# State-space stages of a decoder: softplus chain and row norms on ScalarE and GpSimd, C product one state later, four buffers

## Chip, cores and metric

One core of a Trainium2 chip runs the whole program. The metric is the time of one execution in device microseconds; the engines are TensorE (PE in the profile, PEld its weight loads), VectorE (DVE), ScalarE (ACT), GpSimd (POOL) and SyncE (SP, which issues the DMAs).

## What is computed

The program is a decoder of four layers (twelve blocks) over x of 128 sequences x 64 positions x 128 channels. The change touches one block, the attention of layer 2, which is a selective state-space layer run forwards (m1) and backwards (m2). For each direction, on h = layernorm(layernorm(x)):

```python
xs, z = jnp.split(jnp.einsum('bld,ed->ble', x, in_w), 2, axis=-1)      # 256 channels each
xs = silu(causal_conv_4_taps(xs) + conv_b)
dt, Bc, Cc = jnp.split(jnp.einsum('bld,ed->ble', xs, xproj_w), [8, 24], axis=-1)   # 16 states
dt = jax.nn.softplus(jnp.einsum('blr,dr->bld', dt, dt_w) + dt_b)
dA = jnp.exp(dt[..., None] * A)
dBx = dt[..., None] * Bc[:, :, None, :] * xs[..., None]
# scan over the positions: h = dA_t * h + dBx_t;  y = sum over states of h * C_t
y = (y + Dp * xs) * silu(z)
return jnp.einsum('bld,od->blo', y, out_w)
```

## The kernel before

`mamba` (L1689) is called twice, with `first` true for m1. It works on 16 groups (`C.NG`) of 512 rows (8 sequences of 64 positions). The 256 channels are two halves of 128 partitions (`NHF` 2), the 512 rows lie along the free axis. A group has 16 states (`NS`). All engines run their own hand-written instruction streams, ordered by semaphores; each has a loop of 8 turns with two groups in a turn.

The work of state s of a group:

- GpSimd `state` multiplies `dtx` (dt times xs) by the row of B into `dBx[s % 2]` (L1793), 128x1024. B's rows are spread over the partitions by SyncE's DMAs (`spread_B`, L1757), two states to a transfer, four slots.
- ScalarE `state` makes the decays exp(A dt) into PSUM (`ps_dA`, L1960), one 128x504 activation for each half. There are three such banks, so it can be three halves ahead of the scan and no more.
- VectorE `state` (L2072) runs a scan for each half (L2077), drains, waits for C and multiplies the state by C's row in `ps_C` into `yc[s % 2]` (L2083).
- TensorE waits for `yc`, then spreads C of the next state (`spread_C`, L1872, one bank) and adds `yc` to `ps_y` with four matmul instructions by the identity (`add_state`, L1887).

Beside state s of group i each engine has `front(i + 1, s, ...)`, the preparation of the next group, spread over the states by number. TensorE: gate products at s 2, low-rank products at 3, step sizes (`dt_done`) at 6, transposes at 8, convolution at 10 to 13. ScalarE: silu(z) at 4, copies of `low` and `parts` at 6, exp at 9, copy of rows at 10, ln and exp at 12; silu of xs between states 0 and 1 (`activate`). VectorE: the three-part split of C at 5 (L2044 to L2050), bias, x and -|x| at 7 (L2054, L2057), max(x, 0) and (e+1)-1 at 10 (L2060, L2061), x + ln at 12 (L2065), the last subtraction at 13 (L2069); row normalisation (`normalise`, L2033) at 4 and, in m1, the first normalisation into Y at 14 (L2105). GpSimd: two products of the softplus correction at 11 and 12 and `dtx` at 15. `AHEAD = 2` states of the next group are done at the end of a group. Between them VectorE multiplies `ps_y` by silu(z) (L2109) and adds the projected rows to Y (L2112).

On every engine the order within a state is first `state(i, s)`, then `front(i + 1, s)`, except on TensorE, where `front(i + 1, s)` comes first and then the wait for `yc` of state s:

```python
                        front(i + 1, s, 1 - par, True)
                        if s == 9:
                            skip(par)
                        pe.wait_ge(yc_ready, i * NS + s + 1)
                        spread_C(to, its)
                        add_state(s)
```

## Time and profile before

| | us |
|---|---|
| median of 3 runs | 11680.44 (11670.45 to 11685.3) |
| the profiled execution | 11666.28 |
| its span, first to last instruction | 11664.5 |
| m1, from its first load to that of m2 | 4701.85 to 6062.85 |
| m2, to the start of the joining stage | 6062.85 to 7383.65 |

Busy over the whole span are TensorE 74%, VectorE 67%, ScalarE 34% and GpSimd 21%, but twelve blocks with different limits are mixed in this. The change is confined to 4701.85 to 7383.65 us, so only that stretch is to be read. There a timeline of each engine and the table of waits are the useful views: a row of the timeline gives start, duration, engine, line, operation, names and count, and in brackets the idle time before it and what ended it.

### The profile page before, as it was taken

To read this page: it belongs to the slowest core of one execution; us is meant where nothing else is said; L and a number is where in the kernel's file an instruction comes from. 1 tells how busy PE (TensorE), PEld (TensorE's weight loads), DVE (VectorE), ACT (ScalarE), POOL (GpSimd) and SP (SyncE) were. 2 spreads that over 40 slices of the span, in tenths; PEclk is the share of its full clock that TensorE was granted. 3 is DMA by queue.
4 is the path that set the end of the run, shared out by engine and by line. 5 is a ranking of instruction groups with operands and counts; after the bars stand their busy time and mean duration, and the time that the engine had idled before them with its cause. 6 is when DMAs were issued, how large, how long until landed. Compare 5 with 4: busy or idle time off the path is not lost. (4 is left out here: it accounts for less than half of the span.)

```text
span 11664.5 us, 161252 instructions
## 1 busy us (share of the span) xinstructions
PE 8604.9 (74%) x60164; PEld 5385.6 (46%) x60164; DVE 7794.8 (67%) x11203; ACT 3961.3 (34%) x5327; POOL 2427.5 (21%) x805
## 2 busy tenths in 40 slices
PE   5666888756766747677767777788668888876789
PEld 4444555433445432232223333455445666664566
DVE  6655324567777864788878888555775666666644
ACT  3333213311111025444444444533333333333333
POOL 0000000025445620455545555100000000000000
PEclk7777666667767767888888888899669999997589
DMA  0000000000000000111111111000000000000000
GB/s 18 0 9 7 4 1 0 1 14 0 0 0 0 0 8 0 50 51 52 53 46 53 56 53 55 11 11 8 0 0 17 2 2 2 2 6 6 6 8 14
DMA packets 83306, 183.24 MB, mean 16 GB/s; under 512 B 16107, under 2 KB 38231, under 8 KB 82199
## 3 DMA queue, kind: packets, MB, share of 16 engines
q1 hardware_dynamic: 82966, 178.64, 4.7%
q8 instruction: 223, 3.65, 0.1%
q14 instruction: 117, 0.95, 0.0%
HBM read 171.20 MB, written 7.41 MB: 15 GB/s over the span
## 5 line engine op out<-in xcount | busy, mean ns | idle before, releaser
L1784 POOL TENSOR_TENSOR m_dBx<-m_dtx,m_Bs 128x1024 f32<-128x1024 f32 x516 | 1246.9, 2419 | 863.0 <-DVE m_hs L2077 840.0
L2077 DVE TENSOR_TENSOR_SCAN m_hs<-m_ps_dA,m_dBx 128x512 f32<-128x512 f32 x1032 | 1203.0, 1207 | 189.9 <-POOL m_dBx L1784 139.2
L1889 PE MATMUL m_ps_y<-m_yc,ident 128*128 128x512 f32 x2064 | 1197.1, 711 | 0.0
L1960 ACT ACTIVATE m_ps_dA<-m_dt,m_A 128x504 f32<-128x504 f32 x1032 | 689.1, 679 | 1387.6 <-DVE m_hs L2077 1377.0
L2418 PE MATMUL x_ps_p<-Y,ident 128*128 128x256 f32 (+1 forms) x1920 | 713.5, 547 | 384.4 <-DVE Y L2335 214.8
L2418 PEld LDWEIGHTS x_ps_p<-Y,ident 128*128 128x128 f32 x1920 | 425.7, 242 | 664.7 <-issue 241.5
L2083 DVE TENSOR_TENSOR m_yc<-m_hs,m_ps_C 128x1024 f32<-128x1024 f32 x516 | 630.2, 1221 | 96.4 <-issue 88.0
L1872 PE MATMUL m_ps_C<-m_parts,m_sel 128*128 128x512 bf16 x518 | 229.1, 442 | 616.5 <-DVE m_yc L2083 615.9
L1889 PEld LDWEIGHTS m_ps_y<-m_yc,ident 128*128 128x128 f32 x2064 | 465.5, 227 | 379.3 <-issue 355.4
L547 POOL MEMSET c_vbd<- 128x1152 f32 x2 | 2.1, 1062 | 2939.5 <-POOLq L56 2939.5
L2341 POOL TENSOR_TENSOR Y<-x_score,x_v 128x1024 f32<-128x1024 f32 (+1 forms) x72 | 471.8, 6585 | 243.1 <-DVE x_most L2721 159.6
L1872 PEld LDWEIGHTS m_ps_C<-m_parts,m_sel 128*128 128x128 bf16 x518 | 51.2, 99 | 1007.0 <-DVE m_yc L2083 971.6
L352 PE MATMUL c_ps_t<-ident,c_s 128*128 128x128 f32 x1024 | 238.6, 394 | 233.5 <-ACT c_s L526 233.5
L2341 DVE TENSOR_TENSOR Y<-x_score,x_v 128x1024 f32<-128x1024 f32 (+1 forms) x72 | 375.7, 5254 | 4.3 <-PE x_ps_p L2418 4.3
L2335 POOL TENSOR_TENSOR Y<-x_qk 128x2048 f32<-128x2048 f32 x48 | 305.4, 6392 | 102.8 <-DVE x_most L2711 89.2
L352 PEld LDWEIGHTS c_ps_t<-ident,c_s 128*128 128x128 f32 x1024 | 173.1, 201 | 266.7 <-issue 224.7
L352 PE MATMUL a_ps_t<-ident,a_s 128*128 128x128 f32 x1024 | 218.1, 367 | 87.6 <-ACT a_s L526 87.6
L1127 PEld LDWEIGHTS f_ps_o<-f_w,f_hid 128*128 128x128 f32 x2048 | 246.4, 192 | 65.9 <-issue 46.0
L1339 PE MATMUL a_ps_o<-a_pT,a_val 64*64 64x128 f32 x4096 | 257.9, 277 | 19.3 <-ACT a_pT L1436 19.3
L1324 PE MATMUL a_ps_t<-ident,a_s 128*128 128x128 f32 x1024 | 141.7, 283 | 165.6 <-DVE a_s L1481 152.0
L526 ACT ACTIVATE c_s<-c_s 128x2048 f32<-128x2048 f32 x64 | 122.1, 1908 | 412.3 <-DVE c_s L631 412.3
L1352 PE MATMUL a_ps_out<-a_wo,a_oT 128*128 128x128 f32 x2048 | 256.5, 280 | 0.0
(690 smaller groups left out, 19445.1 us busy)
## 6 DMA issues: line engine op xcount, KB each, us to landing
m_Bs<-m_B_rows SPq DMA_DIRECT2D x258, 512.0 KB, 3.6
c_kvb<-in_ctxT SPq DMA_DIRECT2D x50, 256.0 KB, 2.5
out_dram<-X SPq DMA_DIRECT2D x1, 4096.0 KB
m_B_rows<-m_low SPq DMA_DIRECT2D x34, 32.0 KB, 3.2
c_table<-in_table SPq DMA_DIRECT2D x2, 512.0 KB
focus_rows<-X SPq DMA_DIRECT2D x2, 512.0 KB, 9.5
x_xb<-in_ctx SPq DMA_DIRECT2D x1, 1024.0 KB, 14.8
x_xa<-focus_rows SPq DMA_DIRECT2D x1, 1024.0 KB, 7.1
```

The source lines that it names most:

```text
L352: last = nc.tensor.transpose(ps_t[:, m % 2, t * P:(t + 1) * P], s1[:, u, m // 2, h:h + 2, :].rearrange("p h k -> p (h k)"), C.ident[:])
L1339: last = nc.tensor.matmul(ps_o[r, t, :].rearrange("p (j q) -> p j q", q=P)[:, js, S * b:S * b + S], val[r, q, hg * NK + k, :], pT[r, t, js ...
L1352: last = nc.tensor.matmul(ps_out[:, t, :], oT[:, t, j, :], wo[:, hg * NJ + j, :], start=hg == 0 and t == 0 and j == 0, stop=end and not cr ...
L1784: return nc.gpsimd.tensor_tensor(to, one, other, ALU.mult)
L1872: nc.tensor.matmul(ps_C[:], sel[:, s, :], parts[:, par, :], start=True, stop=True).then_inc(C_done, 1)
L1889: last = nc.tensor.matmul(ps_y[:, m, :], C.ident[:], yc[:, s % 2, m, :], start=s == 0, stop=s == NS - 1)
L1960: nc.scalar.activation(seqs(ps_dA[:, h % 3, :]), seqs(dt[:, par, m, :]), ACT.Exp, scale=A[:, m, s:s + 1]).then_inc(decay, 1)
L2077: nc.vector.tensor_tensor_scan(h[:, m, :], ps_dA[:, (2 * s + m) % 3, :], dBx[:, s % 2, m, :], 0.0, ALU.mult, ALU.add).then_inc(scanned, 1)
L2083: nc.vector.tensor_tensor(yc[:, s % 2, :, :], h, bc(ps_C[:].unsqueeze(1), both), ALU.mult).then_inc(yc_ready, 1)
L2335: return eng.tensor_tensor(to.rearrange("p (q k d) -> p q k d", q=queries, k=ck), bc(qk[:, 0, q:q + queries, :].unsqueeze(2), [P, queries, ...
L2341: last = eng.tensor_tensor(to[:, r * ck * D:(r + 1) * ck * D].rearrange("p (h e k) -> p h e k", h=NH, e=HD), bc(s[:, q + r, :, :].unsqueez ...
L2418: last = nc.tensor.matmul(sum_bank(c)[:, 0:width], C.ident[:], parts[:, :, e], start=e == 0, stop=e == n - 1)
```

## The change

Ring sizes: `AHEAD` goes from 2 to 3, `dBx` and `hs` get four buffers each in place of two, `ps_dA` keeps three banks and `yc` two. VectorE's `state` is split in `scan(j, s)` and `weigh(j, s)`; `weigh` of state s - 1 stands behind `scan` of state s, without a drain. Softplus: TensorE's sums are read by ScalarE (Abs and Relu with the bias, at s 7), exp(-|x|) and 1 + e at 8, ln, 1 - v and exp(-ln) at 9; GpSimd does the four sums and products that follow at s 10 to 13 and `dtx` at 14. `normalise` and the first normalisation become ScalarE activations (s 6 and 13). TensorE's gate products move from s 2 to 3 and the low-rank products from 3 to 4; ScalarE's copies move from 6 to 5. Initial marks are written to a small tile, and ScalarE waits for `scaled` at the start.

```diff
@@ sizes
-    AHEAD = 2
-    SLOTS, CHUNK = 4, 2
-    FREE_HALVES, FREE_STATES = 3, SLOTS * CHUNK
+    AHEAD = 3
+    SLOTS, CHUNK, BX, HS = 4, 2, 4, 4
+    FREE_HALVES, FREE_STATES, FREE_ROWS = 3, SLOTS * CHUNK, 1
...
-        dBx, hs, yc = (sb(n, [P, 2, NHF, GT]) for n in ("dBx", "hs", "yc"))
+        dBx = sb("dBx", [P, BX, NHF, GT])
+        hs, yc = sb("hs", [P, HS, NHF, GT]), sb("yc", [P, 2, NHF, GT])
@@ gpsimd
-                pool.wait_ge(scanned, j * (2 * NS) + (2 * s - 2 + FREE_HALVES))
+                if s >= BX or not in_prologue:
+                    pool.wait_ge(scanned, j * (2 * NS) + (2 * s - 2 * BX + 2 + FREE_HALVES))
...
-                if s == 11:
-                    pool.wait_ge(v_ready, j + 1)
+                if s == 10:
+                    pool.wait_ge(excess, j + 1)
                     hold()
-                    nc.gpsimd.tensor_tensor(v[:], v[:], e[:], ALU.subtract)
+                    nc.gpsimd.tensor_tensor(v[:], v[:], e[:], ALU.add)
                     pool.drain()
+                elif s == 11:
+                    multiply(v[:], v[:], r[:])
                 elif s == 12:
-                    pool.wait_ge(r_ready, j + 1)
-                    hold()
-                    multiply(v[:], v[:], r[:]).then_inc(excess, 1)
-                elif s == 15:
-                    pool.wait_ge(dt_ready, j + 1)
-                    hold()
+                    nc.gpsimd.tensor_tensor(dt[:, par, :, :], x[:], ln[:], ALU.add)
+                    pool.drain()
+                elif s == 13:
+                    nc.gpsimd.tensor_tensor(dt[:, par, :, :], dt[:, par, :, :], v[:], ALU.add).then_inc(dt_ready, 1)
+                    pool.drain()
+                elif s == 14:
                     multiply(dtx[:, par, :, :], dt[:, par, :, :], xs[:, par, :, :])
@@ tensor
-                if s == 2:
+                if s == 3:
                     gate(j, 0)
...
-                elif s == 3:
+                elif s == 4:
                     low_products(j, par)
...
-                        pe.wait_ge(yc_ready, i * NS + s + 1)
+                        pe.wait_ge(yc_ready, i * NS + (s + 1 + FREE_ROWS))
@@ scalar
+            def normalise(j):
+                for p in range(TPG):
+                    n = j * TPG + p
+                    last = nc.scalar.activation(xn[:, p, :], C.X[:, n, :], ACT.Identity, scale=C.RS2[:, bass.ds(n, 1)],
+                                                bias=C.NM2[:, bass.ds(n, 1)])
+                last.then_inc(xn_ready, 1)
...
-                elif s == 6:
+                elif s == 5:
                     act.wait_ge(dbl_done, j + 1)
...
+                elif s == 7:
+                    act.wait_ge(dt_done, j + 1)
+                    for m in range(NHF):
+                        nc.scalar.activation(e[:, m, :], bank[m][:], ACT.Abs, bias=dt_b[:, m:m + 1])
+                    for m in range(NHF):
+                        last = nc.scalar.activation(x[:, m, :], bank[m][:], ACT.Relu, bias=dt_b[:, m:m + 1])
+                    last.then_inc(x_ready, 1)
+                elif s == 8:
+                    act.drain()
+                    nc.scalar.activation(e[:], e[:], ACT.Exp, scale=-1.0)
+                    act.drain()
+                    nc.scalar.activation(v[:], e[:], ACT.Identity, bias=1.0)
                 elif s == 9:
-                    act.wait_ge(neg_ready, j + 1)
-                    nc.scalar.activation(e[:], e[:], ACT.Exp).then_inc(e_ready, 1)
+                    act.drain()
+                    nc.scalar.activation(ln[:], v[:], ACT.Ln)
+                    act.drain()
+                    nc.scalar.activation(v[:], v[:], ACT.Identity, scale=-1.0, bias=1.0)
+                    nc.scalar.activation(r[:], ln[:], ACT.Exp, scale=-1.0).then_inc(excess, 1)
                 elif s == 10:
                     copy_rows(j + 1)
-                elif s == 12:
-                    act.drain()
-                    nc.scalar.activation(ln[:], e[:], ACT.Ln, bias=1.0)
-                    act.drain()
-                    nc.scalar.activation(r[:], ln[:], ACT.Exp, scale=-1.0).then_inc(r_ready, 1)
-
+                elif s == 6 and in_loop:
+                    act.wait_ge(xT_done, j + 1)
+                    normalise(j + 1)
+                elif s == 13 and first and in_loop:
+                    first_norm(j - 1)
@@ vector
+            def scan(j, s, in_prologue=False):
+                if s >= HS or not in_prologue:
+                    dve.wait_ge(yc_ready, j * NS + (s - HS + 1 + FREE_ROWS))
                 dve.wait_ge(dBx_ready, j * NS + (s + 1 + FREE_STATES))
...
+            def weigh(j, s, wait_free=True):
+                dve.wait_ge(scanned, j * (2 * NS) + (2 * s + NHF + FREE_HALVES))
                 if wait_free:
                     dve.wait_ge(y_added, j * NS + (s - 1))
                 dve.wait_ge(C_done, j * NS + (s + 1))
...
                     for s in range(AHEAD, NS):
-                        state(i, s)
+                        scan(i, s)
+                        weigh(i, s - 1)
                         front(i + 1, s, 1 - par)
...
-                    state(i + 1, 0)
+                    scan(i + 1, 0)
+                    weigh(i, NS - 1)
+                    scan(i + 1, 1)
                     dve.wait_ge(y_added, i * NS + NS)
                     nc.vector.tensor_tensor(q[:], sz[:, par, :, :], ps_y[:], ALU.mult).then_inc(y_ready, 1)
-                    state(i + 1, 1)
+                    weigh(i + 1, 0)
+                    scan(i + 1, 2)
+                    weigh(i + 1, 1)
                     dve.wait_ge(out_done, i + 1)
```

In VectorE's stream the blocks for s 7, 10, 12 and 13, both normalisations and the drain at the end of a turn are gone; only the split of C at s 5 is left in its `front`.

## Rows read from the trace of the kernel before

**Rows 1.** The page: its first line, then busy time of each engine.
```profile
span 11664.5 us, 161252 instructions
PE 8604.9 (74%) x60164; PEld 5385.6 (46%) x60164; DVE 7794.8 (67%) x11203; ACT 3961.3 (34%) x5327; POOL 2427.5 (21%) x805
```
**Rows 2.** Table of waits, 4757 to 6060 us: total us, times, longest.
```profile
ACT m_ps_dA L1960 <- DVE m_hs L2077: 709.1, 312, 6.2
POOL m_dBx L1784 <- DVE m_hs L2077: 440.6, 192, 5.7
DVE m_hs L2077 <- POOL m_dBx L1784: 69.7, 34, 5.2
```
**Rows 3.** VectorE's timeline: L2109, first and last of 16, in m1, then m2.
```profile
4837.80 1.21 DVE L2109 TENSOR_TENSOR m_e<-m_sz,m_ps_y 128x1024 f32<-128x1024 f32 x1
...
6052.89 1.22 DVE L2109 TENSOR_TENSOR m_e<-m_sz,m_ps_y 128x1024 f32<-128x1024 f32 x1
6197.64 1.22 DVE L2109 TENSOR_TENSOR m_e<-m_sz,m_ps_y 128x1024 f32<-128x1024 f32 x1
...
7373.89 1.22 DVE L2109 TENSOR_TENSOR m_e<-m_sz,m_ps_y 128x1024 f32<-128x1024 f32 x1
```
**Rows 4.** VectorE's timeline in one group of m1.
```profile
5009.10 2.33 DVE L2077 TENSOR_TENSOR_SCAN m_hs<-m_ps_dA,m_dBx 128x512 f32<-128x512 f32 x2
5011.61 1.22 DVE L2083 TENSOR_TENSOR m_yc<-m_hs,m_ps_C 128x1024 f32<-128x1024 f32 x1 [0.18 <-issue]
5012.75 2.33 DVE L2077 TENSOR_TENSOR_SCAN m_hs<-m_ps_dA,m_dBx 128x512 f32<-128x512 f32 x2
...
5022.15 0.69 DVE L2044 TENSOR_TENSOR m_low<-m_ps_j,m_parts 64x512 f32<-64x512 f32 x1
...
5024.83 2.34 DVE L2077 TENSOR_TENSOR_SCAN m_hs<-m_ps_dA,m_dBx 128x512 f32<-128x512 f32 x2
...
5088.39 2.34 DVE L2077 TENSOR_TENSOR_SCAN m_hs<-m_ps_dA,m_dBx 128x512 f32<-128x512 f32 x2 [3.19 <-issue]
```
**Rows 5.** ScalarE's timeline in the same group, the front of state 12.
```profile
5048.86 1.28 ACT L1992 ACT_TABLE_LOAD   x1
5050.16 1.06 ACT L1992 ACTIVATE m_ln<-m_e 128x1024 f32<-128x1024 f32 x1
5051.27 1.28 ACT L1994 ACT_TABLE_LOAD   x1
5052.56 1.06 ACT L1994 ACTIVATE m_r<-m_ln 128x1024 f32<-128x1024 f32 x1
5053.52 1.87 ACT L1960 ACTIVATE m_ps_dA<-m_dt,m_A 128x504 f32<-128x504 f32 x3
```
**Rows 6.** Timeline of m1's start: a table load ahead of a wait, the first scan.
```profile
4732.49 1.28 ACT L1987 ACT_TABLE_LOAD   x1
...
4740.55 1.06 ACT L1987 ACTIVATE m_e<-m_e 128x1024 f32<-128x1024 f32 x1 [6.77 <-DVE m_e L2057]
...
4756.99 2.34 DVE L2077 TENSOR_TENSOR_SCAN m_hs<-m_ps_dA,m_dBx 128x512 f32<-128x512 f32 x2 [5.16 <-POOL m_dBx L1784]
```
**Rows 7.** Groups by line: Silu, m1 (busy, mean ns); then one line's instructions, Relu elsewhere.
```profile
L1978 ACT ACTIVATE m_sz<-m_ps_j 128x512 f32<-128x512 f32 x16 | 9.6, 597 | 0.2
L1047 ACT ACTIVATE f_hid<-f_ps_h,f_wib x64: 687/687/687, 1289.6 to 1650.1; 128x512 f32<-128x512 f32 x64
```
**Rows 8.** TensorE's timeline: the same four instructions at both clocks.
```profile
5044.11 1.88 PE L1889 MATMUL m_ps_y<-m_yc,ident 128*128 128x512 f32 x4
...
5075.77 3.62 PE L1889 MATMUL m_ps_y<-m_yc,ident 128*128 128x512 f32 x4
```
**Rows 9.** GpSimd's timeline: two products in a row; one behind a drain.
```profile
4754.62 4.64 POOL L1784 TENSOR_TENSOR m_dBx<-m_dtx,m_Bs 128x1024 f32<-128x1024 f32 x2 [0.26 <-issue]
...
5049.79 2.36 POOL L1784 TENSOR_TENSOR m_dBx<-m_dtx,m_Bs 128x1024 f32<-128x1024 f32 x1 [0.31 <-issue]
```
**Rows 10.** ScalarE's timeline in the joining stage: row normalisations, 128x128 with two pointer operands.
```profile
7385.26 3.18 ACT L2135 ACTIVATE mj_xn<-X,NM,RS 128x128 f32 x8
```

More of the change, by code:

```diff
@@ L1768, in _ @@
             store_B(C.NG, 0)
-            spread_B(C.NG, 0, 0)
+            for c in range((AHEAD + CHUNK - 1) // CHUNK):
+                spread_B(C.NG, 0, c)
         n_prepared = 2
@@ L1784, in multiply, with state @@
                 return nc.gpsimd.tensor_tensor(to, one, other, ALU.mult)
-            def state(j, s, par):
+            def state(j, s, par, in_prologue=False):
                 slot = s // CHUNK % SLOTS
@@ L1911, in _ @@
                 front(-1, s, 1, False)
-            for s in range(2, 14):
+            for s in range(3, 14):
                 front(0, s, 0, False)
@@ L1937, in _ @@
             for m in range(NHF):
-                nc.tensor.matmul(ps_y[:, m, :], C.ident[:], yc[:, 1, m, :], start=False, stop=True)
+                nc.tensor.matmul(ps_y[:, m, :], C.ident[:], yc[:, (AHEAD - 1) % 2, m, :], start=False, stop=True)
         @block.scalar
@@ L1947, in _, with first_norm @@
             seqs = lambda t: t.rearrange("p (s n) -> p s n", n=S)[:, :, 1:]
+            def normalise(j):
[4 more added lines that the diff above has]
+                last.then_inc(xn_ready, 1)
+            def first_norm(i):
+                for p in range(TPG):
+                    n = i * TPG + p
+                    last = nc.scalar.activation(C.Y[:, n, :], C.X[:, n, :], ACT.Identity, scale=C.RS[:, bass.ds(n, 1)],
+                                                bias=C.NM[:, bass.ds(n, 1)])
+                last.then_inc(Y_ready, 1)
             def copy_rows(j):
@@ L2012, in _ @@
                     activate(i + 2, par, True)
-                    state(i + 1, 1, 1 - par)
+                    for s in range(1, AHEAD):
+                        state(i + 1, s, 1 - par)
         @block.vector
@@ L2031, in _ @@
             dve.drain()
-            def normalise(j):
-                for p in range(TPG):
-                    n = j * TPG + p
-                    last = nc.vector.tensor_scalar(xn[:, p, :], C.X[:, n, :], C.RS2[:, bass.ds(n, 1)],
-                                                   C.NM2[:, bass.ds(n, 1)], ALU.mult, ALU.add)
-                last.then_inc(xn_ready, 1)
             def front(j, s, par):
@@ L2076, in state @@
                     dve.wait_ge(decay, j * (2 * NS) + (2 * s + m + 1))
-                    nc.vector.tensor_tensor_scan(h[:, m, :], ps_dA[:, (2 * s + m) % 3, :], dBx[:, s % 2, m, :], 0.0, ALU.mult,
-                                                 ALU.add).then_inc(scanned, 1)
-                dve.drain()
+                    nc.vector.tensor_tensor_scan(hs[:, s % HS, m, :], ps_dA[:, (2 * s + m) % 3, :], dBx[:, s % BX, m, :], 0.0,
+                                                 ALU.mult, ALU.add).then_inc(scanned, 1)
+            def weigh(j, s, wait_free=True):
+                dve.wait_ge(scanned, j * (2 * NS) + (2 * s + NHF + FREE_HALVES))
                 if wait_free:
@@ L2082, in state @@
                 dve.wait_ge(C_done, j * NS + (s + 1))
-                nc.vector.tensor_tensor(yc[:, s % 2, :, :], h, bc(ps_C[:].unsqueeze(1), both), ALU.mult).then_inc(yc_ready, 1)
-            normalise(0)
-            dve.drain()
-            dve.wait_ge(xT_done, 1)
-            normalise(1)
-            for s in range(5, 14):
-                front(0, s, 0)
+                nc.vector.tensor_tensor(yc[:, s % 2, :, :], hs[:, s % HS, :, :], bc(ps_C[:].unsqueeze(1), both),
+                                        ALU.mult).then_inc(yc_ready, 1)
+            front(0, 5, 0)
             for s in range(AHEAD):
-                state(0, s, False)
+                scan(0, s, True)
+                if s:
+                    weigh(0, s - 1, False)
             with dve.Fori(0, C.NG // 2) as pair:
@@ L2096, in _ @@
                     for s in range(AHEAD, NS):
[L2097 removed]
+                        scan(i, s)
+                        weigh(i, s - 1)
                         front(i + 1, s, 1 - par)
[L2099 to L2107 removed]
+                    scan(i + 1, 0)
+                    weigh(i, NS - 1)
+                    scan(i + 1, 1)
                     dve.wait_ge(y_added, i * NS + NS)
                     nc.vector.tensor_tensor(q[:], sz[:, par, :, :], ps_y[:], ALU.mult).then_inc(y_ready, 1)
[L2110 removed]
+                    weigh(i + 1, 0)
+                    scan(i + 1, 2)
+                    weigh(i + 1, 1)
                     dve.wait_ge(out_done, i + 1)
+                    if first:
+                        dve.wait_ge(Y_ready, i + 1)
                     nc.vector.tensor_tensor(rows(C.Y, i), ps_k[:].rearrange("p (t d) -> p t d", d=D), rows(C.Y, i),
                                             ALU.add).then_inc(out_read, 1)
[L2114 removed]
+            weigh(C.NG, AHEAD - 1)
 def mamba_join(C, name):
```

58 lines of the change are left out of this document (17 added, 41 removed).

## The prediction

> **What bounds the kernel now.** The page gives 67% for VectorE over the span [rows 1], a mean over twelve blocks; only the two state-space stages matter. I read the table of waits of m1 first. ScalarE and GpSimd wait for VectorE's scans for 709 and 441 us, VectorE for GpSimd for 70 us [rows 2]: VectorE is the engine that the others follow. Then VectorE's timeline. L2109 runs once a group, so its starts give the period: (6052.89 - 4837.80) / 15 = 81.0 us in m1 and (7373.89 - 6197.64) / 15 = 78.4 us in m2 [rows 3]. A state takes 12.75 - 9.10 = 3.65 us: two scans 2.33, a hole of 0.18 behind the drain, the product with C 1.14 from start to start [rows 4]. 16 x 3.65 = 58 us; the other 20 to 23 us of a group are VectorE's share of the front, GpSimd's late dBx (70 / 16 = 4.4) and, once in two groups, 3.19 us at the turn of the loop [rows 4].
>
> **What is taken from VectorE.** The drain goes: 2 x 1.13 + 1.14 = 3.40 a state, 54.4 a group. Left are the split of C (5024.83 - 5022.15 = 2.7 [rows 4]), the product L2109 (1.1 to the next start [rows 3]) and the row add L2112, half its elements (0.6, estimated from that row). VectorE's own work falls to 54.4 + 2.7 + 1.1 + 0.6 = 58.8 us a group. If it stayed the bound, that would be the period. The question is what waits end late instead, and I go by the order of each queue.
>
> **How far ScalarE may be away.** `ps_dA` still has three banks; only `dBx` and `hs` have become deeper. The second decay of state s can start when the first scan of state s - 1 ends (call it t). From t VectorE has the second scan, a product, two scans and a product of its own, 1.13 + 1.14 + 2.26 + 1.14 = 5.67, less 0.07 of overlap: it wants the first decay of state s + 1 at t + 5.60. ScalarE spends 0.05 + 0.62 on the second decay of s and 0.69 + 0.06 on that of s + 1 (duration and spacing from the three in a row [rows 5]; 0.05 to 0.07 is the hand-over between engines). So about 4.2 us of front per state are free. What exceeds it stops the scans. Four places exceed it:
>
> **(a) Silu of z, s 4.** The gate products now come at TensorE's s 3, after the matmuls of state 2, whose product on VectorE now stands behind the scans of state 3. It ends at t + 2.28. TensorE then spreads C (0.07 + 0.23), adds the state (1.72) and does two gate products (1.72, latency 0.16; four instructions start to start are 1.71 at the full clock [rows 8]): z is done at t + 6.18. Behind it on ScalarE come one silu (0.05 + 0.60 [rows 7]), a table load (0.02 + 1.28 [rows 5]) and the decay (0.75): t + 8.9 against 5.6, **3.3 us** of stall. The load of the silu table itself is hidden, since a load is executed ahead of the wait: 4732.49 against 4740.55 [rows 6]. Before, gate was at s 2 and its input one product earlier, so nothing waited.
>
> **(b) Step sizes, s 7.** VectorE read them before; now ScalarE does, and its decays of state 8 are queued behind. By the same steps (product of state 5, C, add, `dt_w` products) `dt_done` is at t + 6.18; then 0.05, two Abs and two Relu at 0.60 from start to start (0.687 each [rows 7]), the decay 0.75: t + 9.4 against 5.6, **3.8 us**.
>
> **(c) exp, ln, exp(-ln), s 8 and 9.** After (b) VectorE starts each scan as its decay comes, so all ScalarE's work counts: from scan 8's first start 0.5 to the end of the second decay, drain 0.1, exp 1.04, drain 0.1, 1 + e 0.95, two decays 1.3, load 1.28 + 0.1, ln 1.06, drain 0.1, 1 - v 1.06, load 1.28, exp 0.95, decay 0.75: 10.7 us until scan 10 can begin [rows 5]. VectorE needs 2 x 3.40 = 6.8: **3.9 us**.
>
> **(d) GpSimd, s 10 to 14.** Its queue stands at s 10 waiting for `excess`, which comes 0.6 us before scan 10; `dBx` 10 is the last it has made, so the four buffers are empty of anything ahead. From there each state needs a dBx and a front operation: 2.32 + 2.35 + 0.31 behind a drain [rows 9], 4.98 a state (4.64 for the one without a drain), against VectorE's 3.40. dBx 11 is 1.1 late, then 1.2 and 3 x 1.6: **7.1 us**. GpSimd's total, 21 operations or 50 us, fits in a group; its late start doesn't. Every moved sum counts here: before, three operations stood in this queue, now five.
>
> **(e) Silu of xs, states 0 and 1.** Two loads and two silus between two decays (3.9 us), with one scan less of allowance (`back` is 2 for the first two halves): **0.9 us**.
>
> The row norms are covered: 3.18 / 8 = 0.40 each [rows 10], 1.6 us at s 6 and at s 13, under the 4.2 us. Their cover gone, they would cost 1.6. Moving the copies to s 5 only follows the low products (0.5 wait, behind (a)). SyncE's stores and spreads have the first need of B's next rows 50 us after the copy; nothing is queued behind them. The bigger AHEAD lets three dBx be made at the group's end, which refills GpSimd's ring before scan 0.
>
> Sum: 3.3 + 3.8 + 3.9 + 7.1 + 0.9 = 19.0; 58.8 + 19.0 = 77.8. The turn of the loop stays, 3.19 less the drain's share of some 0.4, over two groups 1.4: 79.2. **The clock:** TensorE is now inside (a) and (b). [...] That costs between 0 and 3.65 us at each of (a) and (b), 7.3 in all; I take 3.0, nearer to nothing in (a), about 2 in (b). **Period 82.2 us, in both stages**, since Y's norm (m1 only) is no longer VectorE's.
>
> Against before: 15 x (82.2 - 81.0) + 15 x (82.2 - 78.4) = 18 + 57 = 75. The prologue is a bare chain: four norms ahead of the first copy (1.6), Abs and Relu against bias and negation, a table load that was hidden behind a wait [rows 6], two more ScalarE passes, four GpSimd operations of 2.35 to 2.66 in place of two and two on VectorE: I get the first scan 10.5 us later than now (4756.99 [rows 6]); the end has one more state to close, 3.5. 2 x 14 = 28. Total +103 on the profiled execution's 11666.28. The median of the runs is 14.2 above that: **11783 us**.
>
> [...] Rows first: each of ln and exp(-ln) has its own load of 1.28 us [rows 5]. [...]
>
> **Rivals.**
> - *The stalls at their least (same time).* TensorE stays at the full clock where it counts: period 79.2, 15 x (-1.8 + 0.8) + 28 = +13, 11693. [...]
> - *ScalarE's waits are covered (faster).* If the gate and step-size products are done before ScalarE asks, because VectorE's product of the state before is issued sooner than I place it, (a) and (b) vanish: it decides when they are done by t + 2.9 and t + 2.4 in place of t + 6.2. Period 79.2 - 7.1 = 72.1: 15 x (-8.9 - 6.3) + 28 = -200, 11480. With all stalls gone it would be 60.2 and 11120. For it: VectorE loses over 15 us of work a group. Against: three banks.
> - *TensorE slow in both chains (much slower).* All of 7.3: period 86.5, 15 x (5.5 + 8.1) + 28 = +232, 11912.
> - *The change does not do what it says*: the wait merely moves from VectorE's front to its decays; at equal periods only the 28 us of both ends are left, 11708. This lies between the first two cases of the sum and takes no chance of its own.
>
> **How the numbers follow.** My forecast (periods 80.5 to 84.5, that is 11732 to 11852) 0.60; least stalls 0.16; covered waits 0.16; slow chains 0.08. A measurement of this kernel can tell 0.2%, 23 us, from no change: 11657 to 11704 counts as the same. Slower is 0.60 + 0.08 = 0.68, the same 0.16, faster 0.16. The range of 8 in 10 leaves out the covered waits and half of the slow chains: 11650 to 11880.
>
> **What would show it.** In the table of waits of m1 VectorE's scans should wait for the decays (L1960's line) some 12 to 15 us a group and for dBx about 7; ScalarE should wait for the gate and step-size products about 4 and 6 us a group; GpSimd should stand some 16 us before its first sum. Both stages should have the same period. Wrong would be: waits of ScalarE on TensorE near nothing (then it is faster), or a period of m1 that is 2.4 above that of m2.

## The result, and the profile after

The changed kernel takes 11763.67 us (median of four runs, 11755.23 to 11767.75) against 11675.44 for the kernel before (11669.89 to 11685.3): a ratio of 1.0074, with a 95% interval of 1.0056 to 1.0091. It is slower. The forecast was 11783, or +103 on the profiled execution; the two profiled spans differ by 11753.4 - 11664.5 = 88.9. The first line of the page after and its busy times:

```profile
span 11753.4 us, 161630 instructions
...
PE 8599.0 (73%) x60174; PEld 5387.5 (46%) x60174; DVE 7428.4 (63%) x10767; ACT 4193.4 (36%) x5743; POOL 2545.9 (22%) x875
```

VectorE does 366 us less than in [rows 1] and the kernel is slower all the same. Where the time came is seen first from the starts of the blocks, in SyncE's timeline (start, duration, line). After:

```profile
4705.28 0.33 SPq L1749 DMA_DIRECT2D m_g<-in_m_g  x1
...
6082.17 0.33 SPq L1749 DMA_DIRECT2D m_g<-in_m_g  x1
...
7505.80 0.33 SPq L2194 DMA_DIRECT2D m_g<-in_m_g  x1
...
9008.79 0.34 SPq L1271 DMA_DIRECT2D a_wq<-in_a_wq  x1
...
10560.90 0.33 SPq L305 DMA_DIRECT2D c_wq<-in_c_Wq  x1
```

and before:

```profile
4701.85 0.33 SPq L1748 DMA_DIRECT2D m_g<-in_m_g  x1
...
6062.85 0.33 SPq L1748 DMA_DIRECT2D m_g<-in_m_g  x1
...
7434.72 0.33 SPq L2180 DMA_DIRECT2D m_g<-in_m_g  x1
...
8937.55 0.34 SPq L1271 DMA_DIRECT2D a_wq<-in_a_wq  x1
...
10472.27 0.33 SPq L305 DMA_DIRECT2D c_wq<-in_c_Wq  x1
```

Differences of neighbouring rows, after less before: m1 1376.9 - 1361.0 = +15.9, m2 1423.6 - 1371.9 = +51.8, the next block +0.2, the attention block of layer 3 1552.1 - 1534.7 = +17.4, what follows +0.3, what stands ahead of m1 +3.4. So 67.7 of the 88.9 come from the two changed stages, and 21 from code that is the same in both kernels.

The 17.4 of layer 3 stand in one place. TensorE's waits in that block (9008.8 to 10560.9 us in after) have a row, once in each turn of its loop, that the kernel before doesn't have:

```profile
PE a_ps_t L1292 <- issue: 17.0, 15, 1.5
```

The same row, 15.6 to 17.5 us, stands in the profiles of three of the kernels below (step sizes early, softplus back with the places of after, norms back on VectorE), whose block takes 1550.6 to 1551.8 us. It is in none of the other nine, whose block takes 1531.6 to 1536.7. So, as far as one profile of each can show, these 17 us go with the program, and why is open. Where a kernel below is compared with after and doesn't have that row, 15 to 20 us of the difference lie there and not in the changed stages.

The period is read at the product with silu of z (L2119 after, L2109 in [rows 3]), VectorE's timeline, first and last of m1 and of m2:

```profile
4853.60 1.19 DVE L2119 TENSOR_TENSOR m_e<-m_sz,m_ps_y 128x1024 f32<-128x1024 f32 x1
...
6069.41 1.20 DVE L2119 TENSOR_TENSOR m_e<-m_sz,m_ps_y 128x1024 f32<-128x1024 f32 x1
...
6229.16 1.20 DVE L2119 TENSOR_TENSOR m_e<-m_sz,m_ps_y 128x1024 f32<-128x1024 f32 x1
...
7441.93 1.20 DVE L2119 TENSOR_TENSOR m_e<-m_sz,m_ps_y 128x1024 f32<-128x1024 f32 x1
```

(6069.41 - 4853.60) / 15 = 81.05 us in m1 and 80.85 in m2, against 81.0 and 78.4 before: alike in both stages, as forecast, and 1.2 below the forecast of 82.2. The waits of m1 (4770 to 6090 us; total, times, longest) name what VectorE has got in place of its own work:

```profile
ACT m_ps_dA L1979 <- DVE m_hs L2092: 384.0, 201, 4.5
...
POOL m_v L1805 <- ACT m_r L2021: 300.7, 16, 19.5
DVE m_hs L2092 <- ACT m_ps_dA L1979: 233.1, 64, 7.6
...
DVE m_hs L2092 <- POOL m_dBx L1786: 139.7, 81, 30.6
...
ACT m_e L2007 <- PE m_ps_k L1872: 137.8, 16, 9.3
ACT m_sz L1997 <- PE m_ps_j L1859: 52.2, 16, 3.3
```

The scans now wait for the decays 233.1 / 16 = 14.6 us a group, a wait that [rows 2] doesn't have. One group of m1 in VectorE's timeline shows the stalls, each ahead of its scan:

```profile
5029.75 1.19 DVE L2100 TENSOR_TENSOR m_yc<-m_hs,m_ps_C 128x1024 f32<-128x1024 f32 x1
5034.20 2.34 DVE L2092 TENSOR_TENSOR_SCAN m_hs<-m_ps_dA,m_dBx 128x512 f32<-128x512 f32 x2 [3.25 <-ACT m_ps_dA L1979]
...
5055.02 2.34 DVE L2092 TENSOR_TENSOR_SCAN m_hs<-m_ps_dA,m_dBx 128x512 f32<-128x512 f32 x2 [7.57 <-ACT m_ps_dA L1979]
...
5065.53 2.34 DVE L2092 TENSOR_TENSOR_SCAN m_hs<-m_ps_dA,m_dBx 128x512 f32<-128x512 f32 x2 [3.63 <-ACT m_ps_dA L1979]
...
5070.07 2.34 DVE L2092 TENSOR_TENSOR_SCAN m_hs<-m_ps_dA,m_dBx 128x512 f32<-128x512 f32 x2 [1.09 <-POOL m_dBx L1786]
...
5097.26 2.34 DVE L2092 TENSOR_TENSOR_SCAN m_hs<-m_ps_dA,m_dBx 128x512 f32<-128x512 f32 x2 [0.86 <-ACT m_ps_dA L1979]
...
5105.58 0.69 DVE L2126 TENSOR_TENSOR Y<-m_ps_k,Y 128x512 f32 x1 [0.39 <-PE m_ps_k L1888]
5106.30 2.34 DVE L2092 TENSOR_TENSOR_SCAN m_hs<-m_ps_dA,m_dBx 128x512 f32<-128x512 f32 x2
```

These are (a) silu of z, (b) step sizes, (c) the functions exp, ln and exp(-ln) with their table loads, the first of five waits of (d) for GpSimd (the others are 1.17, 1.51, 1.54 and 1.50), and (e) silu of xs. Over the 15 periods of m1 (b) isn't the same in each: it is 7.6 in eleven and 5.2 in four, 6.9 on average; the others hardly vary. The last two rows are the turn of the loop. TensorE's timeline in (b):

```profile
5044.15 0.61 PE L1877 MATMUL m_ps_C<-m_parts,m_sel 128*128 128x512 bf16 x1 [4.34 <-DVE m_yc L2100]
5044.55 3.62 PE L1894 MATMUL m_ps_y<-m_yc,ident 128*128 128x512 f32 x4
5048.10 2.07 PE L1872 MATMUL m_ps_j<-m_low,m_dt_w 8*128 8x512 f32 x2
```

After 4.34 us idle the four adds take 3.62, the longer of the two durations in [rows 8], and from 5044.15 to 5051.80 us the granted clock is 0.50; at the adds of 5037.93 us, which take 1.88, it is 1.00. ScalarE has to wait for TensorE's step sizes behind these slow matmuls. In the kernel before the longer of [rows 8] stands behind an idle time of 3.37 us:

```profile
5075.37 0.61 PE L1872 MATMUL m_ps_C<-m_parts,m_sel 128*128 128x512 bf16 x1 [3.37 <-DVE m_yc L2083]
5075.77 3.62 PE L1889 MATMUL m_ps_y<-m_yc,ident 128*128 128x512 f32 x4
```

From 5075.70 to 5079.40 us the granted clock is 0.50 there, and 1.00 at the 1.88 of [rows 8].

### The profile page after: what moved, and what is told of

It reads as the page before. It is cut to its first block and busy times, and to the rows that moved or that the text cites. A ratio compares the mean times of both kernels' runs of the same rounds, so it can differ in the third digit from the quotient of the medians.

```text
span 11753.4 us, 161630 instructions
## 1 busy us (share of the span) xinstructions
PE 8599.0 (73%) x60174; PEld 5387.5 (46%) x60174; DVE 7428.4 (63%) x10767; ACT 4193.4 (36%) x5743; POOL 2545.9 (22%) x875
## 3 DMA queue, kind: packets, MB, share of 16 engines
q8 instruction: 223, 3.65, 0.1%
## 5 line engine op out<-in xcount | busy, mean ns | idle before, releaser
L1786 POOL TENSOR_TENSOR m_dBx<-m_dtx,m_Bs 128x1024 f32<-128x1024 f32 x518 | 1210.3, 2354 | 413.7 <-DVE m_hs L2092 403.7
L1894 PE MATMUL m_ps_y<-m_yc,ident 128*128 128x512 f32 x2072 | 1163.1, 690 | 0.0
L1436 ACT ACTIVATE a_pT<-a_ps_t 128x1024 f32<-128x1024 f32 x128 | 131.0, 1023 | 373.7 <-PE a_ps_t L1324 373.7
```

What stands on the lines that cost most here:

```text
L1786: return nc.gpsimd.tensor_tensor(to, one, other, ALU.mult)
L1894: last = nc.tensor.matmul(ps_y[:, m, :], C.ident[:], yc[:, s % 2, m, :], start=s == 0, stop=s == NS - 1)
```

## The experiments

All ratios are to the kernel before, with 95% intervals. "After" in a heading means that the edit is made to the changed kernel.

### Step sizes one state earlier, on the kernel after

The theory: ScalarE's wait at (b) is long because TensorE's `dt_w` products stand behind the adds of state 5. The rival: the product of VectorE or ScalarE's own passes set the time, and moving TensorE's product does nothing.

```diff
-                elif s == 6:
+                elif s == 5:
                     step_sizes(j)
```

> The changed kernel with one edit: TensorE's step-size products stand at state 5 in place of 6, so that they no longer follow the add of state 5. Theory of the queues: stall (b), 7.6 us a group in the changed kernel's trace, goes but for some 0.5, since the products are done before ScalarE asks; the other stalls stay, (a) 3.3, (c) about 3.8, (d) about 7. Period 81 -> 75 (less some 1 us of table switches and clock elsewhere: 74 to 75.5), whole kernel 11764 - 32 x 6 = about 11570. Rival 'ScalarE and GpSimd simply have too much work a group': nothing is taken off any engine, period and time stay at 81 and 11764. Rival 'TensorE's clock': the time changes by no more than the clock's part of (b), 3.7 us a group, 11645.

11500.86 us, 0.985 [0.9833, 0.9866], so 263 less than after, more than expected. The period of m1 falls to 73.1, by 8.0. Waits of m1:

```profile
DVE m_hs L2092 <- POOL m_dBx L1786: 139.8, 81, 30.6
DVE m_hs L2092 <- ACT m_ps_dA L1979: 109.8, 52, 3.6
...
ACT m_e L2007 <- PE m_ps_k L1872: 11.8, 7, 2.1
```

The stall (b) is gone but for 0.1, the two of (a) and (c) are left (3.6 is now the longest), and GpSimd's are untouched. That the gain is larger than (b) comes from (c), which falls from 3.62 to 2.7 on average, as ScalarE no longer comes to it late. One line of order in one queue was worth 2.2% of the kernel.

### Gates one state earlier, on the kernel after

The same theory for (a): the gate products are issued at TensorE's s 2 ahead of its wait for that state's product, the low-rank products at 3.

```diff
-                if s == 3:
+                if s == 2:
...
-                elif s == 4:
+                elif s == 3:
...
+                        if s == 2:
+                            front(i + 2, 2, par, True)
```

> The changed kernel with the gate products one state earlier (ahead of the wait for the product of state 2) and the low-rank products at state 3 again. Theory of the queues: stall (a) falls from 3.3 to about 0.7 a group, (b) stays at 7 to 7.6. Period 81 -> 78.5, whole kernel 11764 - 32 x 2.5 = about 11685. Rival 'too much work': no change.

11658.01, 0.9987 [0.9977, 0.9996]: 106 less than after. The period falls by 3.45 to 77.6; the stall that goes is 3.25, and the scans' waits for the decays fall from 233.1 to 181.1 over m1. In the two stages together the gain is 94 us; 19 of the 106 are the row of layer 3.

### Both, on the kernel after

> Both edits of the two kernels before. Theory of the queues: (a) about 1 and (b) under 0.5 are left, (c) may shrink to 2.5 as ScalarE no longer arrives late at it, (d) about 7 stays. Period about 71.5 in both stages, whole kernel 11764 - 32 x 9.3 = about 11465, 1.8% under the kernel before. If the stalls merely moved on to the next wait, the sum of both edits would be worth less than the larger alone.

11388.27, 0.975 [0.9734, 0.9766]: 375 less than after, where the two alone gave 263 + 106 = 369. In the two changed stages alone it is 350, against 249 + 94 = 343. The two stalls don't hide one another. Of the waits of m1 only small ones for the decays are left (54.9 / 39 = 1.4 us each):

```profile
DVE m_hs L2096 <- ACT m_ps_dA L1983: 54.9, 39, 2.6
...
ACT m_e L2011 <- PE m_ps_k L1872: 3.0, 11, 0.5
```

### GpSimd's front one state later as well

If (d) is a matter of where GpSimd stands waiting, then putting its five operations at 11 to 15 in place of 10 to 14 lets it make one dBx more before it waits.

```diff
-                if s == 10:
+                if s == 11:
...
-            for s in range(10, 15):
+            for s in range(11, 16):
```

> As the kernel with both edits, and GpSimd's five front operations at states 11 to 15 in place of 10 to 14, so that dBx of state 11 is made ahead of the wait for excess. Theory of (d): the ring of four holds one dBx more when the wait ends; the stall falls from about 7 to about 3 and moves to states 15 and 0. Period about 68.3, whole kernel about 11360. Rival 'GpSimd is short of throughput in this stretch': the same operations in the same time, (d) stays at 7 and the time equals that of the kernel with both edits.

11319.42, 0.97 [0.9683, 0.9716]: 69 less again. VectorE's timeline, the waits that are left in a group:

```profile
5020.81 2.34 DVE L2096 TENSOR_TENSOR_SCAN m_hs<-m_ps_dA,m_dBx 128x512 f32<-128x512 f32 x2 [0.66 <-POOL m_dBx L1786]
...
5030.91 2.34 DVE L2096 TENSOR_TENSOR_SCAN m_hs<-m_ps_dA,m_dBx 128x512 f32<-128x512 f32 x2 [1.68 <-POOL m_dBx L1786]
...
5038.26 1.22 DVE L2123 TENSOR_TENSOR m_e<-m_sz,m_ps_y 128x1024 f32<-128x1024 f32 x1 [1.65 <-PE m_ps_y L1894]
```

With 1.52 between them the waits for dBx are 3.86 in place of 6.8, and part of what they gave comes back as a wait of 1.65 for TensorE at the group's end. This is why the gain is 2.2 us a group and not 2.9.

### Softplus back on VectorE, on the kernel after, with and without the early placements

Is the move of softplus the loss? The rival to the theory of places says so: ScalarE and GpSimd are the wrong engines for it.

```diff
-                    for m in range(NHF):
-                        nc.scalar.activation(e[:, m, :], bank[m][:], ACT.Abs, bias=dt_b[:, m:m + 1])
-                    for m in range(NHF):
-                        last = nc.scalar.activation(x[:, m, :], bank[m][:], ACT.Relu, bias=dt_b[:, m:m + 1])
...
+                elif s == 7:
+                    dve.wait_ge(dt_done, j + 1)
+                    for m in range(NHF):
+                        last = nc.vector.tensor_scalar(x[:, m, :], bank[m][:], dt_b[:, m:m + 1], None, ALU.add)
...
+                elif s == 12:
+                    dve.drain()
+                    dve.wait_ge(r_ready, j + 1)
+                    nc.vector.tensor_tensor(dt[:, par, :, :], x[:], ln[:], ALU.add)
```

> The changed kernel with one part undone: the softplus chain is back on VectorE, ScalarE (exp at 9, ln and exp at 12) and GpSimd (11, 12, 15) as it was before; the norms stay on ScalarE, the C product stays one state behind, four buffers, gates at 3. Theory of the queues: the wait for the step sizes now stands in VectorE's own queue, behind the same chain of TensorE, some 3 us a group; (a) 3.3 stays, (c) goes, of (d) some 3.5 is left, and VectorE has 8.6 us of work back. Sum 58.5 + 8.6 + 3.3 + 3 + 3.5 + 1 = about 78 in both stages, 11764 - 32 x 3 = about 11665. Rival 'the softplus move is the whole loss, and the late C product and the norms are a clear gain': then this version would lie by their gain, 16 x 0.29 + 2 to 4.5 us of norms + 1.6 for the turn of the loop = 8 to 11 us a group, under the kernel before, about 11370.

> As y1, with the gate and step-size products placed early as in x3. Theory of the queues: (a) falls to about 1 and VectorE's wait for the step sizes to nothing, period about 72, about 11480, so above x3_both (11388) and above x4_both_pool (11319). If the softplus move itself were the loss, this one would be faster than both.

With the chain back on VectorE and the places of after: 11666.72, 0.9989 [0.998, 0.9998], 97 less than after. That is what the theory of places gave (11665), and not the 11370 of the rival. With the chain back and both early placements: 11488.35, 0.9833 [0.9818, 0.9848], which is 100 **more** than the same placements with the chain on ScalarE. So the move of softplus is worth +97 or -100 us according to where TensorE's products stand. The move is sound; its cost was the place. Here the chain is faster off VectorE once TensorE's products are early, and slower while they are late; these runs move the whole chain, its sums to GpSimd, and don't test its operations one by one.

### TensorE kept busy in the stall, on the kernel after

How much of (b) is the clock? Four more calls of matmul (eight instructions in the trace), by a matrix of zeros, add nothing to `ps_y` and keep TensorE at work for 3.60 us in the gap at state 5.

```diff
+                        if s == 5:
+                            for m in (0, 1, 0, 1):
+                                nc.tensor.matmul(ps_y[:, m, :], zero[:], xs[:, par, m, :], start=False, stop=False)
```

> The changed kernel with four extra products by a zero matrix added to ps_y between the low-rank products' state and the wait for the product of state 5, 3.4 us at the full clock, in a stretch in which TensorE stands idle for 4.3 us; the result is unchanged. If the clock is half of stall (b), TensorE stays at its full clock through the add of state 5 and the step sizes, the products take 0.59 each in place of 0.95, and (b) falls from 7.6 to about 4: period 77.4, 11764 - 32 x 3.6 = about 11650. If (b) is the order alone, it stays, and the extra work costs nothing or up to 1 us a group.

11664.26, 0.9983 [0.9974, 0.9993]: more work, and 99 us less than after, of which 75 lie in the two stages and 19 are the row of layer 3. Waits of m1, and (b) in one group of VectorE's timeline:

```profile
DVE m_hs L2097 <- ACT m_ps_dA L1984: 185.7, 64, 4.3
...
ACT m_e L2012 <- PE m_ps_k L1874: 90.3, 16, 6.0
...
5038.96 2.34 DVE L2097 TENSOR_TENSOR_SCAN m_hs<-m_ps_dA,m_dBx 128x512 f32<-128x512 f32 x2 [3.85 <-ACT m_ps_dA L1984]
```

(b) is 3.85 in this group and 3.8 to 3.9 in every period of both stages (4.3 is the first group's, ahead of the loop). The four adds ahead of the step sizes take 1.88 in place of 3.62, and the two pairs of `dt_w` products 1.12 and 1.02 in place of 2.07 and 1.91; the granted clock over them is 1.00 (5031.80 to 5035.75 us) in place of 0.50. So the order alone costs 3.85, for which the forecast had 3.8, and the lower clock 3.7 in most groups and 3.1 on average in m1. The period of m1 falls by 2.5 only, to 78.5: 0.4 of the rest is a new wait of the row add for TensorE's projection, which stood at 0.1.

### The turn of the loop, on the kernel before

The forecast let the hole of 3.19 us in [rows 4] stay, less the drain's own share. VectorE's group ends there with a drain, which the change has removed.

```diff
                     state(i + 1, 1)
...
-                    dve.drain()
```

> The kernel before without VectorE's drain at the end of each group; nothing else. In the changed kernel, which has no such drain, the hole of 3.2 us once in two groups is gone. If the drain is its cause, it goes here too: 1.5 us a group, 32 groups, about 45 us, 11630. If it is the turn of the loop itself and was hidden in the changed kernel by something else, no change beyond 0.2 us a group (11668).

11656.56, 0.9977 [0.9968, 0.9986]: 23 us less, between the two expectations. The hole is gone from the turn, and the wait for dBx that stood behind it shows:

```profile
5080.38 2.34 DVE L2077 TENSOR_TENSOR_SCAN m_hs<-m_ps_dA,m_dBx 128x512 f32<-128x512 f32 x2 [1.44 <-POOL m_dBx L1784]
```

3.19 - 1.44 = 1.75 in one group of two would be 28 us over both stages. The drain by itself isn't the whole cause, though. The scans' waits under "issue" (waits of VectorE on nothing that the profile shows), summed over both stages, are 49.7 us before, 13.1 without the drain, 4.0 with the drain but with the row norms on ScalarE (the run further below), and none in after. Taking away either of the two loses most of it.

### Four dBx buffers alone, on the kernel before

```diff
-        dBx, hs, yc = (sb(n, [P, 2, NHF, GT]) for n in ("dBx", "hs", "yc"))
+        dBx = sb("dBx", [P, BX, NHF, GT])
+        hs, yc = (sb(n, [P, 2, NHF, GT]) for n in ("hs", "yc"))
...
-                pool.wait_ge(scanned, j * (2 * NS) + (2 * s - 2 + FREE_HALVES))
+                    pool.wait_ge(scanned, j * (2 * NS) + (2 * s - 2 * BX + 2 + FREE_HALVES))
```

> The kernel before with four dBx buffers in place of two; nothing else. Theory of the queues: GpSimd's late dBx (4.4 us a group) come from its in-order queue, which stands at its front operations for VectorE and ScalarE with nothing made ahead behind them, and not from the depth of the ring; the time stays within 0.5 us a group, 11680 +- 16. Rival 'depth': the 4.4 us go, 11680 - 140 = about 11540.

11735.07, 1.0053 [1.0035, 1.0071]: slower by 56, which neither theory had. As the queue theory says, the waits for dBx don't fall: they are 4.0 us a group in both kernels. (The 4.4 counts the stage's first wait too: in [rows 2] (69.7 - 5.2) / 16 = 4.0.) What the deeper ring does is let GpSimd run three products one after another, and that costs VectorE something else. Groups by line in m1, first in this kernel,

```profile
L2108 DVE TENSOR_SCALAR Y<-X,RS,NM x64 | 104.3, 1688 | 0.0
```

then in the kernel before:

```profile
L2105 DVE TENSOR_SCALAR Y<-X,RS,NM x64 | 41.0, 699 | 0.0
```

The same 64 instructions last 1.69 us each in place of 0.70: (104.3 - 41.0) = 63 us, and m1 is 1426.4 - 1361.0 = 65.4 longer while m2, which has no such line, is 1.6 shorter.

The kernel before has the same loss at one place already. Its last subtraction, from SBUF to SBUF, starts in each group while a product of GpSimd runs (in one of them at 5387.64 us, beside a product from 5386.52 to 5388.86):

```profile
L2069 DVE TENSOR_TENSOR m_dt<-m_dt,m_v 128x1024 f32<-128x1024 f32 x16 | 37.0, 2312 | 0.0
```

The sum L2065, of the same shape, lasts 1225 ns. The change takes this subtraction from VectorE.

### The row norms back on VectorE, on the kernel after

In after the norms are on ScalarE. If the two engines hinder each other, this is what that part of the change is worth.

```diff
-                elif s == 6 and in_loop:
-                    act.wait_ge(xT_done, j + 1)
-                    normalise(j + 1)
-                elif s == 13 and first and in_loop:
-                    first_norm(j - 1)
...
+                        if s == 4:
+                            dve.wait_ge(xT_done, i + 2)
+                            normalise(i + 2)
+                        elif s == 14 and first:
+                            for p in range(TPG):
+                                n = i * TPG + p
+                                nc.vector.tensor_scalar(C.Y[:, n, :], C.X[:, n, :], C.RS[:, bass.ds(n, 1)],
+                                                        C.NM[:, bass.ds(n, 1)], ALU.mult, ALU.add)
```

> The changed kernel with both row normalisations back on VectorE (after states 4 and 14), as before the change. Theory of the queues: after state 4 VectorE waits 3.3 us for the decays anyway (stall (a)), so the 2.0 us there cost nothing; after state 14 it waits 1.5 us for dBx. Theory of a collision: the version of the kernel before with four dBx buffers shows the Y normalisation (L2108 there) at 1.72 us for one in place of 0.70 while GpSimd works without a pause; here GpSimd does so from state 10 on, so the four take 6.9 us in place of 2.6, less 1.5 absorbed: 5.4 us a group in m1, nothing in m2. Whole kernel 11764 + 16 x 5.4 = about 11850. Without a collision: + 16 x 1.1, about 11780. If VectorE's own work were the bound, + 16 x 4.6 + 16 x 2.0, about 11870, and m2 would be 32 us longer.

11922.86, 1.0214 [1.0197, 1.0231]: 159 more than after. m1 takes 1502.8, +126, and m2 1461.0, +37. VectorE's timeline in one group:

```profile
5023.17 8.53 DVE L2123 TENSOR_SCALAR Y<-X,RS,NM  x4
```

and GpSimd's:

```profile
5022.38 9.24 POOL L1786 TENSOR_TENSOR m_dBx<-m_dtx,m_Bs 128x1024 f32<-128x1024 f32 x4 [0.30 <-DVE m_hs L2090]
```

Four normalisations of 128x128 end with four products of GpSimd, in 8.5 us; their median duration is 2.376 us, that of one product 2.35. The other norms, `x_n`, last 0.67 each (64 of them 38.7 us); in the same group they fall into stall (a), which shrinks from 3.25 to 0.98, so that they are nearly free there; on average (a) is still 1.8 in m1, and they cost some 0.9. The four of the first normalisation are not free: 8.53 a group, less the 1.5 that VectorE waits for dBx at that place in after, is 7.0, so 16 x 7.0 = 112 of m1's 126. Of m2's 37 us 17.2 are the hole at the turn again (the scans' waits under "issue"); in m1 a wait of 1.57 stands there once in two groups, which the profile puts down to GpSimd. In m2 (b) also rises, from 6.8 on average to 7.6 in every group. The collision was taken too low from the run of the four buffers: there GpSimd makes three products in a row, here four, so none of the four norms runs free.

The two timelines agree in number, one norm to each product. GpSimd's side lengthens too: in one group of before the sum L2065 starts at 5056.08 us and lasts 1.23, and the two dBx that GpSimd starts at 5056.11 take 5.70 in place of 4.64 [rows 9]. What the two engines share no run here shows: the form of the instruction wasn't varied.

### The row norms on ScalarE alone, on the kernel before

```diff
+                elif s == 7 and in_loop:
+                    act.wait_ge(xT_done, j + 1)
+                    normalise(j + 1)
+                elif s == 13 and first and in_loop:
+                    first_norm(j - 1)
...
-                        if s == 4:
-                            dve.wait_ge(xT_done, i + 2)
-                            normalise(i + 2)
```

> The kernel before with only the two row normalisations moved to ScalarE (its states 7 and 13). There VectorE is the engine that the others follow, and neither place has a wait behind it, so all of its time comes back: 4.5 us a group in m1, 2.0 in m2, 16 x 6.5 = 104, about 11578. If ScalarE's decays came late by it (1.6 us of front against an allowance of about 4), less.

11536.79, 0.9885 [0.9868, 0.9901]: 138 less than before, with one part of the change only. m1 falls by 88.9 (5.6 a group) and m2 by 47.6 (3.0). The norms of a group were (41.0 + 33.0) / 16 = 4.6 us of VectorE in m1 and 2.1 in m2; the rest, about 1 in each, is the hole at the turn, which goes too. This part alone would have been a gain; what was packed with it turned the sum.

### The version that is best

Both early placements; GpSimd's front at 11 to 15 with x + ln ahead of the operations that need `excess`; 1 - v behind exp(-ln) on ScalarE with a mark of its own; the product L2109 of [rows 3] behind the first product with C, so that it doesn't wait for TensorE.

```diff
-                if s == 10:
+                if s == 11:
...
+                    nc.gpsimd.tensor_tensor(dt[:, par, :, :], x[:], ln[:], ALU.add)
+                elif s == 12:
+                    pool.wait_ge(rest_ready, j + 1)
...
-                    nc.scalar.activation(v[:], v[:], ACT.Identity, scale=-1.0, bias=1.0)
...
+                    nc.scalar.activation(v[:], v[:], ACT.Identity, scale=-1.0, bias=1.0).then_inc(rest_ready, 1)
...
+                    weigh(i + 1, 0)
...
-                    weigh(i + 1, 0)
```

> Both early placements of TensorE's products (as x3_both), GpSimd's five operations at 11 to 15 (as x4_both_pool) with x + ln first, the 1 - v activation moved from ScalarE's state 9 to state 10 under a semaphore of its own, and VectorE's product with silu(z) behind the product of state 0 in place of ahead of it. Theory of the queues, against x4's 68.1 us a group: (c) falls from 2.2 to about 1.1, since 1.06 us leaves ScalarE's longest front; the wait for the last add before L2109 falls from 1.6 to about 0.5; the stall of GpSimd stays at about 3.9. Period about 66, whole kernel 11319 - 32 x 2.1 = about 11250. If these two waits only move on to GpSimd's stretch, no change against x4.

11221.69, 0.9613 [0.9596, 0.963]: 3.9% under the kernel before and 542 us under after. Waits of m1 (4765 to 5823 us):

```profile
DVE m_hs L2098 <- POOL m_dBx L1786: 91.2, 49, 29.6
DVE m_hs L2098 <- ACT m_ps_dA L1985: 24.0, 25, 1.4
```

29.6 of the first is the stage's start; (91.2 - 29.6) / 16 = 3.9 us a group are left for GpSimd, as expected, and 1.5 for the decays. (c) is 1.1, as expected, and the wait ahead of L2109's product falls from 1.3 on average to 0.1. The period of m1 is 64.7, where about 66 was expected.

## Why the prediction was right, and where its terms were off

**The bound.** Right. VectorE's busy time fell by 366 / 32 = 11.4 us a group, and the gaps behind its drains (42.6 us in m1 before, 0.3 after) went as well, and the period of m1 didn't fall: VectorE was the engine that the others followed, and it became one that follows, at five places in ScalarE's and GpSimd's queues. Without the waits at these places the period would be 81.05 - 21.5 = 59.5, against the 58.8 of the forecast. The cadence of a state that isn't stalled is 5027.50 - 5024.15 = 3.35 us, as forecast (3.40).

**The five stalls.** (a) forecast 3.3, measured 3.25. (b) 3.8 before the clock, 6.9 with it on average and 3.85 with TensorE kept busy. (c) 3.9, measured 3.63; its terms as written add up to 10.57 and not 10.7, so it was 3.8. (d) 7.1, measured 1.09 + 1.17 + 1.51 + 1.54 + 1.50 = 6.8. (e) 0.9, measured 0.86. Together 21.5 against 19.0 + 3.0 = 22.0. That these places are the cause, and not the engines, is shown by the early placements: (b) goes but for 0.1 and (a) whole with one state's shift each, and they add up; (d) and (c) shrink as their places are moved.

**The clock.** The sum was right and its split off. I took about 2 in (b) and 1 in (a). It is nothing in (a), whose gate products last 0.59 each (median; the longest 0.70), and in (b) 3.1 on average in m1 by the run that keeps TensorE busy. In two groups of three, the one shown among them, it is 3.7: all four adds and the `dt_w` products ran at the granted clock of 0.50, the upper end of my 0 to 3.65. In the third it is 1.3. So the middle value came out as a mean of two values, and in most groups the whole chain is slow and not part of it. No run shows the 3.0, nor the 3.65 for each place out of which it was taken: they were my estimate, and the runs showed 0 and 3.1 in their place.

**The turn of the loop** is the step that failed. I let the hole stay, at 1.4 us a group. It isn't there in after: 5105.58 + 0.69 = 5106.27, and the next scan starts at 5106.30. 82.2 - 1.4 = 80.8 is the measured period within 0.25. Over 2 x 15 periods the error is 1.2 x 30 = 36 us. The hole was read as a cost of the turn itself; most of it needed the drain and VectorE's row norms together, and the change takes both away. The other terms nearly cancel: the stalls are 0.5 under the forecast and VectorE's own work 0.7 above it.

**The ends.** The first scan comes 4771.28 - 4705.28 = 66.0 us after the stage's start, against 4756.99 - 4701.85 = 55.1 [rows 6]: 10.9 later, forecast 10.5. Both ends of a stage: m1 15.9 - 15 x 0.05 = 15.2, m2 51.8 - 15 x 2.43 = 15.3; forecast 14.

**The total** came nearer than its parts. The stages were to bring +103 and brought +67.7, by the turn of the loop. The other 21 us lie in unchanged code, 17.4 of them in the attention block of layer 3, for which the forecast had no term. They hid more than half of the stages' error of 35 us: that the total is only 15 above the measured +88 is luck to that extent. They aren't scatter between executions, since the wait at L1292 stands in the same four kernels whose block is long and in none of the other ten; their cause stays open. The start of m1, ahead of which nothing was changed, does scatter, between 4698.5 and 4723.7 in the profiled runs.

**What the waits should show** came as said: decays 14.6 us a group (12 to 15), dBx (139.7 - 30.6) / 16 = 6.8 (7), ScalarE for the gates 3.3 (4) and for the step sizes 8.6 (6, by the clock), GpSimd before its first sum 300.7 / 16 = 18.8 (16).

**The table loads.** ln and exp(-ln) each have their load of 1.28 us in after too, and (c) came out by two loads: 3.63 against 3.9, where one load would have made 2.6.

**The rivals.** "Covered waits" needed TensorE's products a state earlier, and with them there the kernel is faster, 11388 against the 11480 that I gave it. The condition wasn't met, and the price was 92 us too small: the period is 69.8 against 72.1, as the hole at the turn is gone (1.4) and (c) is down to 2.2. "Slow chains" was true of one of its two places. "Not what it says", a wait that only moves, was right as a mechanism in m1, where the period moved by 0.05.

**What I missed.** I priced the row norms as VectorE's 4.6 us of work at the durations of before. In the changed kernel they would have cost about twice that in m1, as GpSimd no longer pauses there (8.5 for the four of the first normalisation): their move is worth 159 us there and 138 alone. It didn't enter the forecast, for the sum was built up from what is left on VectorE, and so it did no harm; a forecast made by subtraction from before would have had them too cheap. That the product with C one state late, without its drain, pays for itself wasn't measured alone. Two runs bound it together with the larger rings: the kernels with the chain back on VectorE differ from the one with only the norms moved (11536.79) by these parts and by the places of TensorE's products and ScalarE's copies. With the places of after they are 130 us slower than it (11666.72), with the early placements 48 us faster (11488.35).

## What to carry to other kernels

When an operation is moved to another engine, its own duration can be the small part, as here: ask what that engine has queued behind its wait, where the input stands in the queue of the engine that makes it, and move the producer one state earlier in the same change; here two such shifts were worth 350 us in the changed stages, five times the 68 that the change had lost there. Four dBx buffers in place of two didn't help while GpSimd stood at a wait upstream (the waits for dBx stayed at 4.0 us a group), and they let two engines run at once that hinder each other (1.69 us for a norm in place of 0.70). That a deeper ring doesn't help either while another buffer keeps its depth (three banks of `ps_dA`) was argued here and not varied. Test the parts of a packed change one by one: the row norms were a gain of 1.2% alone, and the move of softplus, at the places it was given, cost 0.8%.

## What the runs showed that I had not expected

- A `tensor_scalar` of VectorE from SBUF to SBUF on 128x128 lasts 0.70 us in the kernel before, 1.69 where GpSimd makes three products in a row, and 2.19 (median 2.38) where it makes four. The scans, which read the decays from PSUM, last the same 2.33 for two in all of them.
- The cast of 64x512 behind stall (a) lasts 0.91 in after, beside a product of GpSimd, against 0.62 in the kernel before and in the one with only the norms moved. That may be the same loss on a small instruction; it wasn't tested.
- VectorE's idle 3.19 us at the turn of the loop came with the drain at the group's end and the row norms on VectorE together: 49.7 us over both stages with both; 13.1 (edit to before) and 17.2 (edit to after, all in m2) with the norms alone, 4.0 with the drain alone, none with neither.
- Matmuls by zeros in TensorE's gap, 3.60 us of extra work a group, made the two stages 75 us shorter: in the stall at (b) 3.1 of 6.9 us were the lower clock.
- The same TensorE code in layer 3 waits 17 us more in some of the programs and not in others, always at one matmul (L1292), though nothing there was changed.
